# K of each head beside zeros in a tile of its own, so that the score products of a fused attention and feed-forward layer span 128 rows instead of 64

## The reference

```python
q = x @ wq.T + bq ; k = x @ wk.T + bk ; v = x @ wv.T + bv        # x is layer-normed, 384 x 1024
q2 = (q @ wiq.T + biq).reshape(N, H, D).transpose(1, 0, 2)         # N=384, H=16 heads, D=64
k2 = (k @ wik.T + bik).reshape(N, H, D).transpose(1, 0, 2)
v2 = (v @ wiv.T + biv).reshape(N, H, D).transpose(1, 0, 2)
scores = jnp.einsum('hnd,hmd->hnm', q2, k2) * scale + mask[None]   # contraction over D=64
attn = jax.nn.softmax(scores, axis=-1)
out = jnp.einsum('hnm,hmd->hnd', attn, v2)
x = x + (out.transpose(1, 0, 2).reshape(N, 1024) @ wo.T + bo)
...
xq = _act_fake_quant(x_normed, clip_x[0])                          # feed-forward, inner width 352
h = _act_fake_quant(jax.nn.silu(gate) * up, clip_down[0])
x = x + jnp.einsum('bsh,ih->...', h, quantised w_down)
```

## Time and profile before

| | |
|---|---|
| runs of the kernel (us) | 333.55, 333.99, 345.47; median 333.99 |
| the profiled execution, its own time (us) | 334.93 |
| its span, first to last instruction (us) | 333.2 |
| busy: PE / DVE / ACT / POOL (us) | 321.6 / 223.8 / 181.9 / 190.8 |
| PE's share of the chain that ended last | 82% |
| score products (L909): 144 matmuls, busy (us) | 15.0 |

### The profile page before, as it was taken

The page is one execution under the profiler, slowest core; times in us unless marked ns, Lnnn a source line. Parts: engine busy times, 40 slices in busy tenths (PEclk is TensorE's granted clock), DMA queues, the critical chain, the costliest instruction groups (busy, mean ns, idle before and its releaser), DMA issues.

```text
span 333.2 us, 5966 instructions
## 1 busy us (share of the span) xinstructions
PE 321.6 (97%) x2071; PEld 295.7 (89%) x2072; DVE 223.8 (67%) x597; ACT 181.9 (55%) x332; POOL 190.8 (57%) x259
## 2 busy tenths in 40 slices
PE   5999999999999999999999999999999999999993
PEld 5899898878999999999999999999999877888852
DVE  3857988856255555514385978879797775497573
ACT  4847257464333333333375968668595865244562
POOL 6686768547777767767926484563726757100004
PEclk9999999999999999999999999999999999999999
DMA  7997434758144333584312141303213110000005
GB/s 257 371 405 279 126 127 147 236 177 251 58 128 126 128 126 126 160 294 134 122 71 66 64 143 48 128 14 115 67 60 128 63 66 0 0 2 0 2 0 191
DMA packets 16827, 41.72 MB, mean 125 GB/s; under 512 B 3504, under 2 KB 7456, under 8 KB 16800
## 3 DMA queue, kind: packets, MB, share of 16 engines
q1 hardware_dynamic: 13088, 38.08, 33.5%
q0 software_dynamic: 2064, 1.80, 1.9%
q10 hardware_dynamic: 1648, 1.48, 1.3%
HBM read 37.99 MB, written 3.37 MB: 124 GB/s over the span
## 4 chain that ended last, share of the span: by engine, by line
PE 82%; DVE 5%; DMA 4%; ACT 3%; POOL 1%; issue 1%; SPq 1%; POOLq 0%; DVEq 0%
PE PS L776 61%; PE PS L933 5%; PE PS L921 5%; PE PS L909 4%; DMA stage<-in_weights 3%; PE PS L757 2%; PE PS L1072 2%; DVE later L1248 1%; DMA V<-in_w_down 1%; PE PS L767 1%; POOL QT L468 1%; DVE fsc L1258 1%; PE PS L810 1%; PE PS L1135 1%; SPq L316 1%
## 5 line engine op out<-in xcount | busy, mean ns | idle before, releaser
L430 POOL TENSOR_TENSOR ring<-stage,ring 128x256 fp32r<-128x256 f32 x124 | 91.0, 772 | 40.7 <-ACT ring L519 37.7
L776 PE MATMUL PS<-XT,ring 128*128 128x384 f32 x528 | 93.3, 335 | 0.0
L776 PEld LDWEIGHTS PS<-XT,ring 128*128 128x128 f32 x528 | 91.4, 188 | 0.1
L448 POOL DMA_INDIRECT codes<-ecol,place x51 | 59.4, 1166 | 25.8 <-DMA codes<-ecol,place 13.8
L519 ACT ACTIVATE ring<-stage 128x1024 fp32r<-128x1024 f32 x52 | 54.3, 1056 | 6.5 <-PE PS L776 3.8
L626 ACT ACTIVATE scratch<-scratch,smx 128x384 f32<-128x384 f32 x48 | 28.9, 605 | 18.5 <-DVE smx L1367 18.5
L776 PE MATMUL PS<-QT,ring 128*128 128x384 f32 x192 | 35.5, 338 | 0.0
L776 PE MATMUL PS<-AT,ring 128*128 128x384 f32 x192 | 35.2, 338 | 0.0
L776 PEld LDWEIGHTS PS<-AT,ring 128*128 128x128 f32 x192 | 33.1, 188 | 1.5 <-issue 1.5
L776 PE MATMUL PS<-ring,AT 128*128 128x512 f32 x144 | 34.1, 393 | 0.0
L1274 DVE TENSOR_TENSOR ring<-stage,ring 128x1024 fp32r<-128x1024 f32 x21 | 25.7, 1226 | 12.1 <-ACT ring L519 12.0
(11 more groups left out here) (202 smaller groups left out, 479.5 us busy)
## 6 DMA issues: line engine op xcount, KB each, us to landing
stage<-in_weights SPq DMA_DIRECT2D x56, 512.0 KB, 3.3
V<-in_w_gate_up SPq DMA_DIRECT2D x4, 512.0 KB, 5.7
codes<-scratch SPq DMA_DIRECT2D x3, 576.0 KB, 14.8
X<-in_x SPq DMA_DIRECT2D x3, 512.0 KB, 4.9
scratch<-codes POOLq DMA_DIRECT2D x2, 576.0 KB, 6.0
scratch<-in_w_gate_up SPq DMA_DIRECT2D x2, 512.0 KB, 6.4
V<-in_w_down SPq DMA_DIRECT2D x5, 176.0 KB, 3.9
codes<-ecol,place POOLq DMA_INDIRECT x51, 3.1
```

The source lines that it names most:

```text
L430: ins = pool.tensor_tensor(ring[1][:, slot, piece], stage[:, slot % STAGE, piece], ring[0][:, slot, piece].bitcast(F32), ALU.subtract)
L448: pool.indirect_dma_start(codes[b].rearrange("(n a) -> n a", a=1), bass.IndirectOffsetOnAxis(ap=place[:, t:t + 1], axis=0), ecol[:, VAL, t ...
L776: ins = pe.matmul(outs, lhs[a], rhs[b], start=start and n == 0, stop=stop and n == 2, skip_group_check=True)
```

## The change

`K2` becomes one pair of tiles (high and low) for each head instead of one pair for both. In head 0's tiles, rows 0 to 63 hold K and rows 64 to 127 hold zeros; in head 1's it is the other way round. The score product of a head then takes all 128 rows of `Q2` as its stationary operand and all 128 rows of that head's K tile as its moving one; the zeros take the other head's features out. The number of matmuls, their order and their 384 columns stay.

The zeros are written once: POOL copies them from `blank` into four half tiles at the start, each copy waited for before the next, between the edge tables and the first low part of the weights. PE waits once for the semaphore `beside_zero` ahead of the first score. K is taken out of PSUM in two instructions of 64 rows on ACT and two on DVE for each pair, where one of 128 rows stood; the semaphore goes up at the second. The scratch tile `later` moves into a part of `wdN` that is written only afterwards, to make room.

```diff
-        K2 = [sb(f"K2{i}", [P, N], F32R) for i in range(2)]
+        K2 = [[sb(f"K2{h}{i}", [P, N], F32R) for i in range(2)] for h in range(2)]
...
-        later = sb("later", [P, 8, P], BF16)
+        later = wdN[:, 4:8, :].rearrange("p a b -> p (a b)")[:, 0:8 * P].rearrange("p (n q) -> p n q", n=8)
...
+            pool.wait_ge(blank_ready, 1)
+            for h in range(2):
+                for i in range(2):
+                    r = ROWS[1 - h]
+                    chain.step(pool.tensor_copy(K2[h][i][r, :], blank[r, 0, :]))
+            pool.sem_inc(beside_zero, 1)
             pool.wait_ge(y_ready, NT + 1)
...
             def k_high(t):
                 act.wait_ge(w_used, 2 * t + (RING + CPAIR + 2))
-                act.activation(K2[0][:, :], PS[:, PROJ + (t < 2), 0:N], ACT.Identity,
-                               bias=bias[:, BIAS_IK + t:BIAS_IK + t + 1]).then_inc(proj_high, 1)
+                for h, r in enumerate(ROWS):
+                    ins = act.activation(K2[h][0][r, :], PS[r, PROJ + (t < 2), 0:N], ACT.Identity,
+                                         bias=bias[r, BIAS_IK + t:BIAS_IK + t + 1])
+                ins.then_inc(proj_high, 1)
...
-                        for h, r in enumerate(ROWS):
-                            ins = pe.matmul(PS[:, score_bank(p, h, m), 0:N], Q2[p % 2][a][r, m * P:(m + 1) * P],
-                                            K2[b][r, :], start=n == 0, stop=n == 2)
+                        for h in range(2):
+                            ins = pe.matmul(PS[:, score_bank(p, h, m), 0:N], Q2[p % 2][a][:, m * P:(m + 1) * P],
+                                            K2[h][b][:, :], start=n == 0, stop=n == 2)
...
             pair_part(34, range(0, 6))
+            pe.wait_ge(beside_zero, 1)
             pe.wait_ge(proj_low, 2 + 26)
             score(0, range(NT))
...
             def k_low(t):
                 dve.wait_ge(proj_high, 2 * t + 26)
-                dve.scalar_tensor_tensor(K2[1][:, :], PS[:, PROJ + (t < 2), 0:N], bias[:, BIAS_IK + t:BIAS_IK + t + 1],
-                                         K2[0][:, :].bitcast(F32), ALU.add, ALU.subtract).then_inc(proj_low, 1)
+                for h, r in enumerate(ROWS):
+                    ins = dve.scalar_tensor_tensor(K2[h][1][r, :], PS[r, PROJ + (t < 2), 0:N],
+                                                   bias[r, BIAS_IK + t:BIAS_IK + t + 1],
+                                                   K2[h][0][r, :].bitcast(F32), ALU.add, ALU.subtract)
+                ins.then_inc(proj_low, 1)
```

More of the change, by code:

```diff
@@ L216, in gnn_ffn @@
         t_low = sem("t_low")
+        beside_zero = sem("beside_zero")
         proj_high = sem("proj_high")
```

## The result

| | before | after |
|---|---|---|
| median of six runs each (us) | 337.58 | 346.36 |
| lowest run (us) | 333.55 | 345.02 |
| the profiled execution: its own time, span (us) | 334.93, 333.2 | 347.92, 345.8 |

The changed kernel is slower: 1.0348 of the time before, 95% interval 1.0313 to 1.0384. The ratio leaves out disturbed executions, of which each side had some; by it the change costs 11.6 us on 334.0, where I had forecast 10.0.

A forecast was written before the change was run, and what follows sets the result against it. PE was taken as the bound, with no hidden waits in the loop. Terms 8.5 + 0.8 + 0.4 + 0.1 + 0.2 = 10.0 us on the 333.99 median gave 344.0 us, 3.0% slower, range 341.3 to 347.3.

The forecast's parts named there:

- score products, all eight: Full-row score products on PE: 1.22 us more for each of seven scores, 8.5 us, and 0.8 for the last pair's.
- waits for K's take-out and behind it: PE waiting for K's PSUM bank, 0.4 us once, and the last pair's score waiting behind `k_low`, 0.1 us.
- zeros and start: POOL's four zero copies fit its hole at the start; DVE's norms held up 0.2 us, between 0 and 1.6.
- two halves side by side: Score products on rows 0 to 63 and 64 to 127 run together, 0.098 us each instead of 0.175.
- the 0.17 us that I read: Price of the 24 matmuls behind a score, 4.36 us instead of 4.19, making a score cost 1.94 us.
- they must be neighbours: In the score, two neighbouring products, one on each half of the rows, run side by side.
- the one on K in two steps: Second half adds 0.48 us on ACT, 0.55 on DVE; PE waits 0.4 us in turn u = 0, elsewhere up to 0.1.
- 0.1 of slack: In turn u = 0, the slower score's later masking and exponentials give 0.1 us back against K's take-out.
- Rival 1: Two-step K take-out becomes the bound: PE waits some 0.4 us more in six turns, + 2.5, 346.5 us; chance 0.12.
- The last pair: Its score waits for pair 6's probabilities, which DVE finishes behind `k_low`: 0.1 us, at most 0.3.
- my estimate was up to 1.6 us: At the start, three DVE norms each held behind one POOL copy of 0.53 us under the exclusive lock.

The follow-up runs named there:

- experiment 2: Kernel before with score products over all 128 rows of its joint K tile, no zeros, no two-step take-out: 344.04 us median, ratio 1.0300.
- experiment 1: Changed kernel with score products back on 64 rows; separate head tiles, zeros and two-step take-out of K stay: 337.01 us median, ratio 1.0079.
- experiment 9: Kernel before with only the four copies of zeros, into tiles nobody reads, and the moved scratch tile: 336.89 us median, ratio 1.0023.
- experiment 4: Kernel before with all 18 products of a score on rows 0 to 63: 346.49 us median, ratio 1.0337.
- experiment 3: Kernel before with, for each row tile, three products of one head, then three of the other: 334.38 us median, ratio 0.9988.
- experiment 5: Kernel before with nine products of one head, then nine of the other: 2.77 us a score; ran once, whole time 351.43 us not used.
- experiment 7: Kernel before with only ACT's half of K's take-out in two 64-row steps, into the joint tile: 340.04 us, ratio 1.0113.
- experiment 6: Changed kernel with ACT's take-out of K ahead of weight chunk 39's high part in turn u = 0: 344.93 us median, ratio 1.0335.
- experiment 8: Kernel before with only DVE's half of K's take-out in two 64-row steps, into the joint tile: 339.67 us, ratio 1.0136.

## Why the prediction came out as it did

The direction, the place and the main mechanism held; the sum was too small, 10.0 us for a measured 11.6 by the ratio. That it came so near is in part luck: the score products cost 0.5 us less than the sum had, K's take-out 1.6 us more.

| term (us) | forecast | shown |
|---|---|---|
| score products, all eight | 8.5 + 0.8 | 8.78 (experiment 2) |
| waits for K's take-out and behind it | 0.4 + 0.1 | 1.55 (experiment 1), about 2.1 with full rows |
| zeros and start | 0.2 | not to be told from 0 (experiment 9) |

*The score products.* A distance of 0.173 us where I had 0.175 to 0.177, and no edges, as forecast: per later turn 1.13 became 1.04 ahead of the score, 1.77 became 3.12, 4.27 became 4.16 behind it, 1.15 us in all where I had 1.22. The reason that I gave, two halves side by side, is shown by experiments 2 and 4 together. Today's edges cost more than the 0.17 us that I read: 0.09 ahead of the score and 0.11 behind it, and another 0.2 us lie inside the 1.77, of which nine distances of 0.173 are 1.56. That they must be neighbours, as I put it, is wrong (experiments 3 and 5).

*The step that failed is the one on K in two steps*: "PE waits about 0.4 us there, once; in the other turns 0, up to 0.1 each". Shown: 2.72 - 1.89 = 0.83 in turn u = 0, and 0.15 in each of the four later turns of the loop. Three numbers in it were too kind. I took 0.48 and 0.55 us for a second half, from operations that overlap; the halves take 0.57 and 0.63, about the upper bound of 0.62 that I had written beside. I counted the 0.11 us of the semaphore as slack. And I gave 0.1 us of slack back for the slower score, of which nothing arrived: the waits with full rows (0.83, 0.15) are no smaller than without (0.79, 0.12). With full rows the waits and what hangs on them come to 2.12 us (10.90 - 8.78) where the sum had 0.5. Rival 1, the take-out as an added bound, was thus right in kind: 1.6 of its 2.5 us came, though not as 0.4 in each turn.

*The last pair.* I allowed 0.1 us there. PE's distances around it, in the changed kernel and in experiment 2, which has no second step: `weigh` comes after 2.99 and 2.82 us, the score after another 1.30 and 1.07, and its first piece takes 2.20 and 2.08. That is 0.53 us more. The score waits for what DVE finishes behind `k_low` there:

```profile
271.42 1.25 DVE L1370 SCALAR_TENSOR_TENSOR K<-PS,bias,K 64x384 fp32r<-64x384 f32 x2
272.84 0.62 DVE L1400 SCALAR_TENSOR_TENSOR XT<-PS,bias,XT 64x384 fp32r<-64x384 f32 x1 [0.17 <-ACT XT L643]
...
274.08 2.88 DVE L1237 TENSOR_TENSOR PT<-PS,PT 128x384 fp32r<-128x384 f32 x6
```

DVE is done at 276.96, and the first score product starts at 277.02 instead of 0.24 us sooner. One more wait was not in my list: behind pair 0, where ACT takes K of pair 1 out ahead of the probabilities, the step is 2.22 instead of 2.06 us, and 2.20 with ACT's half alone (experiment 7).

*The start.* POOL's hole held the copies and DVE was held up, both as forecast in kind. The timelines of POOL and DVE there answer to the earlier trace rows:

```profile
9.64 2.83 POOL L439 CAST K<-scratch 64x384 fp32r<-64x384 f32 x4 [0.17 <-POOL ecol L413]
12.84 1.42 POOL L431 TENSOR_TENSOR ring<-stage,ring 128x256 fp32r<-128x256 f32 x2 [0.36 <-DVE V L1191]
...
9.72 0.43 DVE L1184 SCALAR_TENSOR_TENSOR rs<-rs 128x1 f32<-128x1 f32 x1
11.57 1.19 DVE L1191 TENSOR_SCALAR V<-X,mv,rs 128x512 f32<-128x512 f32 x2
```

The last norms end at 12.76 instead of 12.37: the 128x1 operation under the first copy took 0.43 us, 0.22 before, and the last two norms 1.19, 1.00 before. Experiment 9, with the copies and none of the other work, has the same two (0.44 and 1.19 us), and experiments 2 and 3, without copies, have the 1.00: the copies caused it. It went the other way too: the copy that begins under DVE's norm of 0.81 us (10.65) took 1.05 us, the other three 0.50 to 0.59:

```profile
10.77 1.05 POOL L439 CAST K<-scratch 64x384 fp32r<-64x384 f32 x1
```

Of the 0.39 us little is left further on: the transfer on the chain starts at 16.13 instead of 16.00, and in experiments 1 and 6, which have the same start, the first score comes at 164.90 and 165.06, not after the 165.60 of the kernel before. By the Trainium skill's exclusive lock (SBUF — State Buffer, section SBUF: two separate sides) my estimate was up to 1.6 us; the rows agree with the rule in these three places, where the operation that began second took longer, and DVE lost a quarter of that.

*What stays open.* 10.90 us in the stretch leave 0.7 us of the 11.6 outside it. Experiment 2, which does nothing at the start, has the same sort of rest (1.0300 is 10.0 us, its stretch 8.78). Experiment 4 has it the other way round (1.0337 is 11.3 us, its stretch 166.32, which is 12.1 more). The rest lies ahead of the first score or behind the last maximum. There profiles differ by more than that where their code is the same: 12.27 us from the last maximum to the end in experiment 3, 13.92 in experiment 8. I did not find its cause.

## What to carry to other kernels

Contractions over 64 rows on the two halves of the array are worth keeping apart: the second of two such products came free here, and only a block of them cost some 0.4 us at its edges. Padding them with zeros to 128 rows took a score from 1.77 to 3.12 us. Judge it from the starts of matmuls or from the union of busy time, since the duration of one is nearly the same in both forms. When an operation out of PSUM is cut in two by rows, count a whole operation for each half and the semaphore behind it, and hold that against the slack of whoever waits to reuse the bank, turn by turn: the odd turn, where another task stands ahead, pays most.

## What the hardware showed that I had not expected

- Products on the two halves of the rows run side by side without being neighbours, and start out of the written order: three and three give the full rate (1.77 us for 18), nine and nine give three pairs (2.77), one half alone none (3.32).
- 64 rows alone cost what 128 do, 0.173 us from start to start; a block of 64-row products costs 0.2 us more inside it (0.28 us between its first two starts, 0.27 behind its last) and 0.2 around it.
- Two operations of 64x384 out of PSUM follow each other at 0.57 us on ACT and 0.62 on DVE, their full duration, while six of DVE's of 128x384 stand 0.47 apart at a duration of 0.55.
- ACT can stand in its loop with nothing in the trace to release it, 5.79 us in the changed kernel and up to 17.65 in experiment 7; most of that is absorbed, about 2 us of it reached the first score here.
